# Attention's scores in float32r: q and k split into high and low parts, three products for one

## What is computed

```python
qkv = x @ W_qkv + b_qkv
Q, K, V = ...                       # (16, 512, 16 heads, 64) each
scores = jnp.einsum('bqhi,bkhi->bhqk', Q, K) / jnp.sqrt(64.0)
scores = scores + mask              # -10000 above the diagonal
probs = jax.nn.softmax(scores, axis=-1)
vals = jnp.einsum('bkhi,bhqk->bqhi', V, probs)
x = x + (vals @ W_out + b_out) + ffn(x)   # x on the right is the normalised one
```

## Time and profile before

| | |
|---|---|
| median of 3 runs | 3098.28 us (3098.13 to 3100.84) |
| the profiled execution | 3098.15 us |
| its span, first to last instruction | 3096.4 us |
| TensorE busy | 3034.2 us, 98% |
| weight loads busy | 2061.8 us, 67% |
| VectorE busy | 1986.9 us, 64% |
| ScalarE busy | 1667.5 us, 54% |
| GpSimd busy | 1014.3 us, 33% |
| granted TensorE clock, mean | 0.999 of full speed |

### The profile page before, as it was taken

How to read it: one execution, slowest core, us unless ns; L and a number is a source line. 1 busy time by engine, 2 the same in 40 slices (tenths; PEclk the granted TensorE clock), 3 DMA queues, 4 the chain that set the end, 5 groups by cost and what they waited for, 6 DMA issues and landing times.

```text
span 3096.4 us, 87877 instructions
## 1 busy us (share of the span) xinstructions
PE 3034.2 (98%) x34560; PEld 2061.8 (67%) x34560; DVE 1986.9 (64%) x6942; ACT 1667.5 (54%) x3126; POOL 1014.3 (33%) x987
## 2 busy tenths in 40 slices
PE   7999999999999999999999999999999999999998
PEld 4666666666666666666767666666666676766765
DVE  6576665667576665666666666665766757666564
ACT  4555555545555555555555555555655555555553
POOL 5052432515152341424314243142433405225030
PEclk9999999999999999999999999999999999999999
DMA  3000000000000000000000000000000000000000
GB/s 98 9 2 2 12 2 12 2 12 2 2 12 2 9 5 2 12 2 12 2 2 12 2 12 2 2 12 2 12 2 2 12 2 12 2 2 9 2 9 5
DMA packets 41791, 25.18 MB, mean 8 GB/s; under 512 B 13059, under 2 KB 40621, under 8 KB 41389
## 3 DMA queue, kind: packets, MB, share of 16 engines
q1 hardware_dynamic: 41388, 19.56, 2.3%
HBM read 14.96 MB, written 4.19 MB: 6 GB/s over the span
## 4 chain that ended last, share of the span: by engine, by line
PE 87%; DVE 4%; issue 3%; ACT 3%; POOL 2%; DMA 0%; SPq 0%; POOLq 0%; ACTq 0%; DVEq 0%
PE bank L1157 10%; PE bank L1111 9%; PE bank L1028 7%; PE bank L1201 7%; PE bank L1143 5%; PE bank L1169 3%; PE bank L1217 3%; PE bank L1186 3%; PE bank L1206 3%; PE bank L1021 3%; PE bank L1135 3%; PE bank L1244 3%; PE bank L1022 3%; PE bank L1023 3%; PE bank L1239 2%
## 5 line engine op out<-in xcount | busy, mean ns | idle before, releaser
L884 DVE CUSTOM_DVE_ANT_0 bank<-bank,future 128x128 f32<-128x128 f32 (+3 forms) x1024 | 467.7, 529 | 93.8 <-PE bank L1070 92.8
L755 ACT ACTIVATE probs<-bank 128x512 f32<-128x512 f32 (+1 forms) x768 | 346.6, 531 | 183.2 <-PE bank L1120 183.0
L897 DVE CUSTOM_DVE_ANT_0 bank<-bank,band 128x192 f32<-128x192 f32 x1024 | 331.2, 396 | 162.8 <-PE bank L1088 162.7
L689 POOL TENSOR_TENSOR rnorm<-ssc,minus_half 128x8 f32<-128x8 f32 x256 | 426.8, 1667 | 21.3
L1111 PE MATMUL bank<-Qa,Ka 64*128 64x512 f32 (+3 forms) x2048 | 389.7, 463 | 4.1 <-ACT negT L747 2.3
L687 POOL TENSOR_SCALAR ssc<-ss 128x8 f32<-128x8 f32 x256 | 99.7, 389 | 880.8 <-DVE ss L942 875.8
L1157 PEld LDWEIGHTS bank<-Va,probs 128*64 128x64 f32 x10240 | 316.8, 138 | 84.7 <-issue 66.1
L1157 PE MATMUL bank<-Va,probs 128*64 128x65 f32 x10240 | 346.8, 224 | 0.0
L935 DVE TENSOR_TENSOR scratch<-bank,rope_t 128x512 f32<-128x512 f32 x256 | 176.4, 689 | 237.0 <-ACT scratch L786 196.2
L680 POOL TENSOR_TENSOR lrstd<-lvar,minus_half 128x4 f32<-128x4 f32 x32 | 32.4, 1014 | 874.9 <-DVE lvar L957 874.9
L763 ACT ACTIVATE lprobs<-bank 128x384 f32<-128x384 f32 x512 | 221.5, 489 | 165.5 <-PE bank L1145 153.8
(11 more groups left out here) (154 smaller groups left out, 6843.7 us busy)
## 6 DMA issues: line engine op xcount, KB each, us to landing
x_res<-in_L_attn_x SPq DMA_DIRECT2D x16, 256.0 KB, 3.1
x_rows<-in_L_attn_x SPq DMA_DIRECT2D x16, 256.0 KB, 3.5
out<-yT SPq DMA_DIRECT2D x16, 256.0 KB, 2.4
Lqkv<-in_L_ffn_wqkv SPq DMA_DIRECT2D x2, 768.0 KB, 4.7
rope_t<-in_rope SPq DMA_DIRECT2D x8, 128.0 KB, 4.8
Kf<-in_L_attn_W_qkv SPq DMA_DIRECT2D x1, 768.0 KB, 7.6
Qf<-in_L_attn_W_qkv SPq DMA_DIRECT2D x1, 768.0 KB, 9.2
Lw<-in_L_ffn_w SPq DMA_DIRECT2D x2, 341.0 KB
```

The lines of the kernel that those rows point to most:

```text
L689: g.tensor_tensor(rnorm[s][:, :], ssc[:, :], minus_half[:, :], ALU.pow).then_inc(rnorm_ready.sem, 1)
L755: psum.raise_read(a.activation(probs[j][:, at:at + n], psum.bank(i, task, (u, j))[:, 0:n], ACT.Exp, scale=float(HEAD) ** -0.5), i, task, ( ...
L884: ins = v.tensor_tensor_reduce(psum.bank(i, task, (u, j))[:, at:at + n], psum.bank(i, task, (u, j))[:, at:at + n], future[:, SEQ - n:SEQ], ...
L897: ins = v.tensor_tensor_reduce(psum.bank(i, task, (u, j))[:, k * BAND:(k + 1) * BAND], psum.bank(i, task, (u, j))[:, k * BAND:(k + 1) * BAND],
```

## The change

q and k of a pair are kept as two float32r tiles each, a high part and a low part. ScalarE writes the high part, as it wrote the float32 tile before, but no longer declares the bank read. VectorE gets a new step in a_proj: one scalar-tensor-tensor instruction each for q and k computes bank + bias - high part, writes it as the low part, and declares the bank read. A new semaphore, hi_a_ready, tells VectorE and TensorE of ScalarE's copy; a_max waits on it alone and reads the high parts.

In a_st each product of k and q becomes three: hi x hi, lo of k x hi of q, hi of k x lo of q, summed in the bank. A product is never narrower than 256 columns (`wide`), so key tile 3 is computed for 256 queries instead of 128. Tiles 3 and 2 now share the third bank (tile 3 first, the 128 columns too many are overwritten by tile 2's first product), and the second bank holds tile 1 alone. The STEPS table is given the new step and new lengths for a_st, and a_max needs only step 3 of a_proj, which is ScalarE's copy of k.

```diff
 
-CAUSAL_AT = [0, 512, 1024, 896]
-
-CAUSAL_USES = [(0, 512, [(0, 0)]), (512, 512, [(1, 0), (3, 384)]), (1024, 256, [(2, 0)])]
+CAUSAL_AT = [0, 512, 896, 1152]
+
+CAUSAL_USES = [(0, 512, [(0, 0)]), (512, 384, [(1, 0)]), (896, 384, [(3, 256), (2, 0)])]
 
...
     "xt": [("pe", 0.6, (), (0,), ()), ("act", 0.65, (0,), (), ()), ("dve", 0.75, (1,), (), (0,))],
-    "a_proj": [("pe", 0.85, (), (0,), ()), ("pe", 0.8, (), (1,), ()), ("act", 0.72, (0,), (), (0,)), ("act", 0.72, (1,), (), (1,))],
+    "a_proj": [("pe", 0.85, (), (0,), ()), ("pe", 0.8, (), (1,), ()), ("act", 0.72, (0,), (), ()), ("act", 0.72, (1,), (), ()),
+               ("dve", 0.76, (2,), (), (0,)), ("dve", 0.76, (3,), (), (1,))],
     "a_v": [("pe", 0.83, (), (0,), ()), ("act", 0.62, (0,), (), (0,))],
     "a_max": both([0.3, 0.2, 0.28]) + [("dve", us, (b // 2,), (), (b,)) for b, us in enumerate((0.74, 0.74, 0.52, 0.52, 0.62, 0.62))],
     "a_neg": [("pe", 0.32, (), (0,), ()), ("act", 0.62, (0,), (), (0,))],
-    "a_st": both([1.32, 1.32, 0.66]) + [("act", us, (b // 2,), (), (b,)) for b, us in enumerate((0.72, 0.6, 0.6, 0.6, 0.4, 0.4))],
+    "a_st": both([1.2, 0.9, 0.95]) + [("act", us, (b // 2,), (), (b,)) for b, us in enumerate((0.72, 0.6, 0.5, 0.5, 0.5, 0.5))],
     "a_pv": [("pe", 1.32, (), (0,), ()), ("dve", 0.65, (0,), (), (0,))],
...
     if kind in ("a_max", "a_st"):
-        return [(i, ("a_neg", *at), 99), (i, ("a_proj", *at), 99)] if kind == "a_st" else [(i, ("a_proj", *at), 99)]
+        return [(i, ("a_neg", *at), 99), (i, ("a_proj", *at), 99)] if kind == "a_st" else [(i, ("a_proj", *at), 3)]
     if kind in ("f_neg", "a_neg"):
...
 
-        Qa = [sb(f"Qa{b}", [P, SEQ]) for b in range(2)]
-        Ka = [sb(f"Ka{b}", [P, SEQ]) for b in range(2)]
+        Qa = [[sb(f"Qa{b}_{s}", [P, SEQ], F32R) for s in ("hi", "lo")] for b in range(2)]
+        Ka = [[sb(f"Ka{b}_{s}", [P, SEQ], F32R) for s in ("hi", "lo")] for b in range(2)]
         Va = [sb(f"Va{b}", [P, TILES, 4, HEAD + 1]) for b in range(2)]
...
         sums_ready = Signal(sem("sums_ready"), dict(f_q="q", f_k="k"))
+        hi_a_ready = Signal(sem("hi_a_ready"), dict(a_proj="qk"))
         norm_ready = Signal(sem("norm_ready"), dict(norm="saen"))
...
                     for c, m, whole_of in ((0, "q", Qa), (PAIRS, "k", Ka)):
-                        alone(i, task, m, whole_of[p % 2][:, :], psum.bank(i, task, m)[:, :], ACT.Identity,
-                              bias=bqkv[:, c + p:c + p + 1])
+                        psum.wait_filled(act, i, task, m)
+                        a.activation(whole_of[p % 2][0][:, :], psum.bank(i, task, m)[:, :], ACT.Identity,
+                                     bias=bqkv[:, c + p:c + p + 1]).then_inc(hi_a_ready.sem, 1)
                 elif kind == "a_v":
...
                                                     ALU.subtract), i, task, "x")
+                elif kind == "a_proj":
+                    p = task[1]
+                    if i == 0 and p == 0:
+                        dve.wait_ge(bias_in, 16 * (PAIRS // 4))
+                    for c, m, parts in ((0, "q", Qa), (PAIRS, "k", Ka)):
+                        hi_a_ready.wait(dve, i, task, m)
+                        hi, lo = parts[p % 2]
+                        psum.raise_read(v.scalar_tensor_tensor(lo[:, :], psum.bank(i, task, m)[:, :], bqkv[:, c + p:c + p + 1],
+                                                               hi[:, :].bitcast(F32), ALU.add, ALU.subtract), i, task, m)
                 elif kind == "a_max":
...
                     p = task[1]
-                    psum.wait_all_read(pe, i, task, [(("a_proj", p), m) for m in "qk"])
-                    Q, K = leading(Qa[p % 2][:, :]), leading(Ka[p % 2][:, :])
+                    hi_a_ready.wait(pe, i, ("a_proj", p), "k")
+                    Q, K = leading(Qa[p % 2][0][:, :]), leading(Ka[p % 2][0][:, :])
                     for u, uses in enumerate(MAX_USES):
...
                             end = at + SEQ - k * P
-                            queries = slice(k * P, SEQ)
-                            for j in range(2):
-                                mm(bank[j][:, at:end], Ka[p % 2][HALF[j], tile(k)], Qa[p % 2][HALF[j], queries],
-                                   start=True, stop=False)
+                            wide = max(SEQ - k * P, 2 * P)
+                            for n, (m, w) in enumerate(((0, 0), (1, 0), (0, 1))):
+                                for j in range(2):
+                                    mm(bank[j][:, end - wide:end], Ka[p % 2][m][HALF[j], tile(k)],
+                                       Qa[p % 2][w][HALF[j], SEQ - wide:SEQ], start=(n == 0), stop=False)
                             if k < TILES - 1:
```

## The result

| | before | after |
|---|---|---|
| median | 3098.28 us | 3112.11 us (3110.37 to 3113.39, 5 runs) |
| ratio to before | 1 | 1.0043, 95% interval 1.0029 to 1.0058 |
| profiled execution, its span | 3098.15, 3096.4 us | 3110.37, 3108.6 us |
| TensorE busy | 3034.2 us | 3015.8 us |
| TensorE without a matmul (span less busy) | 62.2 us | 92.8 us |

The change makes the kernel 0.43% slower, where 3084 us and faster was forecast. 3112 lies inside the range of 3052 to 3122.

The account below looks back on a forecast made before the run. TensorE's streaming was taken to bound the steady part, latency only the first 40 and last 35 us. The sum was 3098.15 - 23 (products) + 6 (end) + 3 (start) = 3084 us, 0.45% less, range 3052 to 3122.

Parts of the forecast that it names:

- The products, -23: In a_st, three float32r products replace four float32 passes: 0.18 us less a pair, 23 us less over 128 pairs.
- stream at the clock: Rival: a_st's float32r products on 64 rows run at N/2.4, saving 47 us instead of 23, giving 3060; chance 17%.
- The low parts in the steady part, 0: VectorE's 256 added a_proj instructions, about 191 us of work, cost zero in the steady part, between -10 and +30 us.
- the two reasons given: For zero cost of low parts: VectorE is idle 35% in the steady part; the planner's table names the 0.76 us step.
- The order in the steady part, 0: Between start and end, no separate term for the new task order; steady-part TensorE idle time expected as before.
- VectorE's term: Steady-part cost of waiting for VectorE's low parts, carried at zero, between -10 and +30 us.
- the forecast's sign: TensorE's idle time in 1000 to 3000 us stays as before, some 14 us.
- VectorE's rival: Low parts hold q's and k's banks longer, new waits eat the gain: 3116; sign over 40 us idle; chance 26%.
- The end, +6 (3 to 9): Second layer's last steps, f_wo to f_down, run without attention interleaved: 29 us from f_wo to end, +6 us in all.
- The start, +3 (0 to 6): First tile's f_q, f_k, f_v move later; with about 1.3 us wait at a_neg of pair 1, +3 us.
- The sign that I had named for a wrong forecast: Scores not shortened by 0.1 to 0.4 us a pair, or TensorE's new idle time taking over 14 us of it.
- a case of 3116 us: VectorE's step eats the gain: 0.25 us new waiting a pair from banks held longer, 32 us more; chance 26%.

Follow-up runs that it names:

- e7: Changed kernel with a_st's table lengths set to the traced ones and the planner keeping 120 courses instead of 40: 3078.01 us, ratio 0.9938.
- e2: Code of the kernel before, with the new planner rows and a_max dependence, so in the changed kernel's order: 3132.04 us, ratio 1.0111.
- e3: Changed kernel in its own order without VectorE's low parts, all three products using the high parts: 3109.03 us, ratio 1.0038.
- e6: Changed kernel with key tile 3 computed over its 128 columns instead of 256, same order: 3104.08 us, ratio 1.0019.
- e1: Changed code in the order of the kernel before (old planner rows and old a_max dependence): 3099.09 us, ratio 1.0005.
- e5: Changed code in the order of the kernel before, without low parts, all three products using the high parts: 3078.61 us, ratio 0.994.
- e9: Changed code in the old order, VectorE's two a_proj instructions reading SBUF instead of the bank, ScalarE freeing the bank: 3105.44 us, ratio 1.0025.

## Why the prediction was wrong, step by step

- **The products, -23: right.** 0.18 us a pair in the timeline, and 19 to 23 us in three orders. The choice of the float32r rows over N/2.4 was right; the rival "stream at the clock" did not happen. The Trainium skill ("TensorE: Matmul & The Clock Gate", section "Back-to-back issue gap") gives N/2.4 + 2.5 ns for an isolated matmul and says nothing there of types: "whatever the type" was my reading, and the 0.23 us of 512 float32r columns do not bear it out.
- **The low parts in the steady part, 0: right in the new order, for one of the two reasons given.** 2 to 3 us. That the table names the step is the reason that the runs leave, though three orders, only one of them made without it, are few to rest it on: slack in a bad order is not the reason, since e7's order idles less than 64 us and pays 2 too. VectorE's idle third alone would not have done it: in the old order, with the same third idle, they cost 20.5.
- **The order in the steady part, 0: this is the step that failed.** I carried "a new order can also wait less" as a lower bound of -10 us on VectorE's term, and gave the steady part of the new order no term of its own. It idles 14 us more there, and e2, the old code in this order, idles as long (28.1 us in 1000 to 3000): the order's waits, none of them for a low part, took what the products gained. The 27.6 us of the kernel after in 1000 to 3000 lie between the 14 that I had given as the forecast's sign and the 40 of VectorE's rival. The upper bound of +30 covered it, under the name of another cause. I looked at the new order at the start and the end only, and took the middle, 93% of the run, for unchanged because it repeats.
- **The end, +6 (3 to 9): too small, at +11.2 idle and 3.2 of clock.** The chain alone I put at 29.0 us from rows at full clock; it took 32.7, and the 3.2 us of clock are nearly all of the difference. I had worked out that the layer's steps would come alone, and did not ask what the clock would do in the gaps. That it falls there belongs to this order: over the last 32.7 us e2, e3 and e6, which share it, have the same mean clock as the kernel after, 0.84. In the old order before, e1 and e5 have 1.00 over the last 34.7 us, e9 0.95. And I put what lies ahead of f_wo at 0.3 us, where the wait for q and k of the last layer comes to some 6. I had followed the old order's attention tasks, which moved ahead, to the place they left, but not looked who had stood beside them.
- **The start, +3 (0 to 6): +5.6,** inside its bounds. The wait named was right in place and size (1.12 us against 1.3); a_neg's own of 1.85 us and the longer one for xT_lo were not seen.

The sum with what was measured: 3098.15 - 23 + 5.6 + 13.9 + 11.2 + 1.5 = 3107.4, against 3110.37. The 3.0 us that are missing are in TensorE's busy time: without the clock it fell by 20.0 us (18.5 and 1.5), not by 23, and why is open. All three order terms erred to the same side. The sign that I had named for a wrong forecast is there: the scores are shorter, and new idle time takes 30.6 us, over the 14. The forecast's own 3072 to 3096 were narrower than its terms: with each at its bound the sum runs from 3068 to 3120. I gave 26% to a case of 3116 us, whose time was nearly right and whose mechanism was not the one at work: e3 takes all of VectorE's new step away and gets 3 us back.

## What to carry to other kernels

Where a planner or scheduler makes the order from a table, an edit of the table is a change of its own, to be priced as one and measured apart: run the old code in the new order and the new code in the old. Here that split 14 us of loss into 23 us of gain, 3 of low parts and 34 of order. Before the work inside such a kernel is judged, search the order as widely for both; otherwise one compares two draws. And where a change clears other work from a latency chain on TensorE, count the clock into the chain.

## What the runs showed of the hardware

- Float32r products with 64 rows, two heads side by side, step as one product of the full array does: 0.23 and 0.12 us for 512 and 256 columns in both. 384 columns take 0.18. 128 columns take 0.11, which is also the step of the weight loads.
- TensorE's clock fell to 0.50 in the last chain (3084 to 3094 us) after it had worked 1.66 of the 4 us ahead, and was back at 1.00 in 3098 to 3100. The same chain with other work in its gaps kept 1.00 in three of four kernels. In the kernel before it fell for 3.4 us after 2.50 busy of 4 us.
- VectorE's scalar-tensor-tensor of 128x512 takes 742 to 749 ns with one operand in PSUM, and 745 to 750 ns with all in SBUF, as medians. From SBUF single ones took up to 1.78 us, the one shown beside GpSimd's work, and GpSimd's own row of 1.04 us took 1.59.
